# Shorter convolutions, other first loads and a new order of events in a convolution, attention and expert kernel

## What is computed

```python
x = x + conv(_gn(x))                        # per channel of an image: normalise, add a bias, double both axes,
                                            # 12 x 12 filter, leaky relu * sqrt(2), 12 x 12 filter, every second point
t = tokens(x)                               # (16, 1024, 32)
t = t + attention(_ln_t(t), Wq, Wk, Wv)     # one causal head of width 32 over 1024 tokens
u = _ln_t(t)
probs = softmax(u @ gate_w.T + gate_b, axis=tokens)
topv, topi = top_k(probs, 8)                # 8 tokens for each of 16 experts of an image
pooled = sum(topv * u[topi])                # (16 images, 16 experts, 32)
out = gelu([pooled, 1] @ weight1) ... @ weight2
t = t + scatter_add(topi, topv * out)
```

## Time and profile before

| | us |
|---|---|
| median of 3 runs | 413.75 |
| the profiled execution | 406.51 |
| its span in the trace | 404.6 |
| PE busy in it | 348.4 |
| DVE busy | 310.3 |
| ACT busy | 256.4 |
| POOL busy | 239.8 |
| mean granted clock of TensorE | 0.943 |

### The profile page before, as it was taken

How to read it: one execution, slowest core, us unless ns; L and a number is a source line. 1 busy time by engine, 2 the same in 40 slices (tenths; PEclk the granted TensorE clock), 3 DMA queues, 4 the chain that set the end, 5 groups by cost and what they waited for, 6 DMA issues and landing times.

```text
span 404.6 us, 7839 instructions
## 1 busy us (share of the span) xinstructions
PE 348.4 (86%) x3046; PEld 260.4 (64%) x3046; DVE 310.3 (77%) x559; ACT 256.4 (63%) x343; POOL 239.8 (59%) x141
## 2 busy tenths in 40 slices
PE   1189998999899999999599999999986887969775
PEld 1068876667587776857477677676764535647574
DVE  2888779786969878699868786986998995765521
ACT  0113454797988959788476778898696888830500
POOL 5314564366679698886734989856497974162000
PEclk9999999999999999999789999999998997998755
DMA  3900000000000000000000000000020000000311
GB/s 105 203 1 2 2 0 2 2 3 0 3 3 2 0 2 3 2 1 2 0 2 2 2 2 2 2 2 2 0 56 0 2 0 25 19 0 20 86 52 53
DMA packets 16033, 6.70 MB, mean 17 GB/s; under 512 B 6735, under 2 KB 15869, under 8 KB 15997
## 3 DMA queue, kind: packets, MB, share of 16 engines
q1 hardware_dynamic: 13280, 5.55, 5.3%
q10 hardware_dynamic: 2717, 0.66, 1.1%
HBM read 3.63 MB, written 2.11 MB: 14 GB/s over the span
## 4 chain that ended last, share of the span: by engine, by line
PE 58%; DVE 15%; ACT 10%; issue 9%; DMA 3%; POOL 2%; SPq 1%; ACTq 1%; DVEq 0%; POOLq 0%
PE psB L874 13%; PE psA L874 11%; PE psB L989 5%; ACT Pp L582 5%; PE psA L974 4%; PE psB L1010 4%; PE psA L1018 3%; PE psA L1054 3%; DVE negmax L739 3%; PE psA L864 3%; PE psA L1032 2%; DVE Pp L393 2%; DVE xin L682 1%; PE psB L992 1%; ACT e L581 1%
## 5 line engine op out<-in xcount | busy, mean ns | idle before, releaser
L393 POOL TENSOR_TENSOR Pp<-e,Pp 128x1024 f16<-128x1024 f32 x45 | 107.3, 2393 | 11.7 <-ACT Pp L582 11.5
L739 DVE TENSOR_REDUCE negmax<-psA 128x1 f32<-128x512 f32 (+7 forms) x128 | 90.7, 749 | 18.5 <-PE psA L977 17.6
L581 ACT ACTIVATE e<-psB 128x1024 f32<-128x1024 f32 (+1 forms) x80 | 76.7, 958 | 9.9 <-PE psB L992 4.5
L582 ACT ACTIVATE Pp<-psB 128x1024 f16<-128x1024 f32 (+1 forms) x80 | 77.0, 963 | 0.0
L874 PE MATMUL psB<-xin,UU 128*128 128x224 f16 (+1 forms) x480 | 56.6, 277 | 1.1 <-ACT Pp L582 0.6
L974 PE MATMUL psA<-zK,yQ 128*128 128x512 f16 (+1 forms) x192 | 49.2, 340 | 9.0 <-DVE uT L759 4.9
L989 PE MATMUL psB<-yQ,zK 128*128 128x512 f16 (+1 forms) x192 | 49.2, 335 | 6.9 <-ACT Pp L582 3.7
L874 PE MATMUL psA<-y,DD 128*128 128x224 f16 (+1 forms) x480 | 55.1, 273 | 0.0
L874 PEld LDWEIGHTS psB<-xin,UU 128*128 128x128 f16 x480 | 47.1, 99 | 9.5 <-ACT oT L586 1.5
L874 PEld LDWEIGHTS psA<-y,DD 128*128 128x128 f16 x480 | 46.7, 98 | 5.5
L489 POOL TENSOR_TENSOR y<-y 128x1024 f16<-128x1024 f32 x16 | 36.7, 2291 | 14.1 <-ACT y L547 14.1
(11 more groups left out here) (157 smaller groups left out, 603.7 us busy)
## 6 DMA issues: line engine op xcount, KB each, us to landing
x_all<-in_x_dram SPq DMA_DIRECT2D x4, 512.0 KB, 4.6
out_dram<-x_all SPq DMA_DIRECT2D x8, 256.0 KB, 2.3
yQ<-rows SPq DMA_DIRECT2D x32, 2.0 KB
Pp<-filter_tables ACTq DMA_DIRECT2D x4, 121.9 KB, 3.3
w_halves<-y SPq DMA_DIRECT2D x12, 32.0 KB, 1.8
cst<-shape_constants SPq DMA_DIRECT2D x1, 326.5 KB, 4.2
y<-in_L_ffn_weight_dram SPq DMA_DIRECT2D x4, 64.0 KB, 1.9
xin<-in_L_ffn_weight_dram SPq DMA_DIRECT2D x1, 256.0 KB, 3.4
```

The source lines that it names most:

```text
L393: return engine.tensor_tensor(Pp[:, n % 2, 1, o:o + N], e32[:, (NU * n + i) % 3, 0:N], Pp[:, n % 2, 0, o:o + N], ALU.subtract)
L581: nc.scalar.activation(e32[:, m % 3, 0:N], slot(e)[:, 0:N], ACT.Exp)
L582: nc.scalar.activation(Pp[:, n % 2, 0, UOFF[e[2]]:UOFF[e[2]] + N], slot(e)[:, 0:N], ACT.Exp).then_inc(b_drained, 1)
L739: ins = nc.vector.tensor_reduce(negmax[:, n % 2, m - 1:m], s[:, at:at + P * m], X, ALU.max, negate=True)
```

## The change

1. `up`: the two middle output rows (t of 1 and 2) used a matrix for k = -1 and another for k = 1. Those two each have one half of the partitions that is not zero, so they are one matrix now, applied without a shift to a new tile `mix`: the image with its first 64 partitions moved by one position one way and its last 64 the other way. Eight products, 24 matmuls, 18 of them on 256 columns. UU gets its blocks in places that wrap around (`filter_places`).
2. `mix` is filled by DMAs on SP (four for each of two pieces of a group); of the first image by ACT and DVE copies. DVE clears the edge columns (event `edges`, four memsets a group).
3. `down`: four of the ten products have 64 output columns that are not zero. They are issued as pairs of 64-column tiles, one into partitions 0 to 63 and one into 64 to 127, at the end of the pass: 18 full matmuls and 12 halves.
4. Start: the bias of the convolution gets its own semaphore; the gate's bias and x of group 1 are loaded ahead of the wait for the tables; U is made in three events between the statistics of group 0; UU is filled by three DMAs on SP, one copy on ACT and two on DVE; 12 `keep_busy` matmuls stand ahead of the first `up`.
5. Last group: its logits go from PE to ACT to DVE in two halves; ACT calls an exponential of one element at `uT` 3; scatter 0 stands before `wT` 3.
6. A new STEP, FIRST and LAST. `late` lets a later image keep less lead: `up` runs 9 steps ahead for images 0 to 2, 7 for 3 to 5 and 6 from image 6 (before: 5, with the tail of the same step); `down` 7, 5 and 4 from image 3; `prob` units 0 to 2 of an image stand one step earlier; `pv` 14 stands a step later.

The diff, cut to its core:

```diff
+PRODUCTS = ((0, 0), (0, 1), (1, 0))
+LOW, HIGH = slice(0, P // 2), slice(P // 2, P)
-def batch(ahead, name, *more):
+def batch(ahead, name, *more, late=()):
 
-    return lambda t: (name, t + ahead) + more if 0 <= t + ahead < B else None
+    at = {n - ahead + sum(n >= m for m in late): n for n in range(B)}
+    event = lambda t: (name, at[t]) + more if t in at else None
+    return event
...
-FIRST = [("xT", 0), ("gn_mean", 0), ("gn_var", 0), ("U", 0), ("normalise", 0), ("image", 0), ("UU", 0), ("image_low", 0)]
+FIRST = [("xT", 0), ("U", 0), ("gn_mean", 0), ("U", 1), ("gn_var", 0), ("U", 2), ("normalise", 0), ("image", 0), ("image_low", 0), ("edges", 0)]
...
+STEP = [once(-7, "xT", 1), group(5, "uT"), batch(0, "prob", 3), group(4, "mean", 1), once(-3, "image_low", 1),
+        group(3, "mean", 0), once(-4, "xT", 2), once(-5, "small", 1), batch(1, "shift"), once(2, "image", 3),
+        batch(3, "split_z"), batch(0, "low", 2), once(1, "normalise", 3), group(7, "pool"), once(-5, "image", 1),
+        once(21, "dev", 3, 1), once(14, "w1", 1), once(19, "mean", 3, 1), batch(7, "down", late=(1, 1, 3,)),
+        batch(0, "low", 3), batch(2, "score", 1), once(-3, "gn_mean", 2), group(6, "route"), once(-6, "gn_mean", 1),
+        once(-8, "xT", 3), once(5, "edges", 3), batch(0, "zV"), once(-7, "small", 0), group(4, "dev", 1),
+        batch(8, "y_low", late=(1, 3, 6,)), batch(0, "prob", 4), once(-2, "gn_var", 2), group(5, "logits"),
+        group(3, "dev", 0), group(2, "proj", 0), batch(2, "score", 4), batch(3, "zK"), batch(2, "score", 2),
+        batch(1, "prob", 0), once(3, "image_low", 3), once(-9, "dnT", 0), once(-1, "gn_var", 3), batch(0, "low", 4),
+        once(1, "image_low", 2), batch(1, "low", 0), group(5, "logit_max"), once(-5, "normalise", 1),
+        batch(5, "tok", late=(1,)), batch(2, "score", 3), batch(2, "score", 0), batch(1, "prob", 1),
+        once(-3, "gn_mean", 3), batch(4, "z_rstd"), once(-3, "edges", 1), group(5, "logit_exp"),
+        once(-2, "normalise", 2), batch(0, "pv", late=(14,)), batch(1, "low", 1), once(1, "edges", 2),
+        once(12, "w1", 0), group(6, "wT"), once(-6, "gn_var", 1), batch(3, "yQ"), once(15, "proj", 3, 1),
+        batch(1, "prob", 2), once(-4, "small", 2), group(3, "proj", 1), batch(9, "up", late=(3, 3, 6,)),
+        once(0, "image", 2), group(5, "select")]
+
+LAST = [("hidden", 0), ("proj", G - 1, 2), ("mean", G - 1, 2), ("experts", 0), ("dev", G - 1, 2), ("turned", 0),
+        ("uT", G - 1), ("scatter", 1), ("logits", G - 1), ("logit_max", G - 1), ("logit_exp", G - 1),
+        ("select", G - 1), ("scatter", 2), ("route", G - 1), ("scatter", 0), ("wT", G - 1), ("pool", G - 1),
+        ("hidden", 1), ("experts", 1), ("turned", 1), ("scatter", G - 1)]
...
+        def filter_places(r):
+
+            q, far = slice(C * r, C * r + C), max(0, 2 - r)
+            moves = [(R - 1 - r, R - 1 - r + NS, 0, NS)] + ([(0, far, NS - far, NS)] if far else [])
...
             for b in range(GB):
                 sp.dma_start(gw_sb[:, b, :], gate_w).then_inc(proj_loaded, 16)
+                sp.dma_start(gb_sb[E_ * b:E_ * b + E_, :], gate_b.rearrange("(e a) -> e a", a=1)).then_inc(proj_loaded, 16)
+            sp.dma_start(x_all[:, 1, :].rearrange("p (b a n) -> p b a n", b=GB, a=2), x_tokens[1]).then_inc(x_loaded[1], 16)
             sp.wait_ge(toeplitz_loaded, 16 * R)
...
+            sp.wait_ge(fills_ready, 4)
+            sp.wait_ge(U_split, 2)
+            for r in (0, R - 1):
+                spread_filter(sp, r)
...
+                elif name == "image_low":
+                    if g >= 1:
+                        sp.wait_ge(mix_ready, 4 * g)
+                    if g >= 2:
+                        sp.wait_ge(b_filled, BU["up", GB * (g - 1) - 1] + 1)
+                    for i, (lo, hi) in enumerate(PIECES):
+                        if g == 0 and i == 0:
+                            continue
+                        for part, filled in enumerate((xin_high, xin_ready)):
+                            sp.wait_ge(filled, 2 * g + 1 + i)
+                            image, mixed = img[g % 2][part], mix[:, g % 2, part, :]
+                            sp.dma_start(mixed[0:P // 2, lo:hi - 1], image[0:P // 2, lo + 1:hi]).then_inc(mix_moved[i], 16)
+                            sp.dma_start(mixed[P // 2:P, lo + 1:hi], image[P // 2:P, lo:hi - 1]).then_inc(mix_moved[i], 16)
...
                     if g == 0 and i == 0:
-                        pool.wait_ge(filters_loaded, 48)
+                        pool.wait_ge(bias_loaded, 16)
...
+            act.wait_ge(fills_ready, 4)
+            act.wait_ge(U_split, 2)
+            place_to, place_from = filter_places(2)[0]
+            nc.scalar.activation(place_to, place_from, ACT.Copy).then_inc(UU_copied, 1)
...
+                    if n == G - 1:
+                        cut = BANK
+                        act.wait_ge(logits_half, n + 1)
+                        nc.scalar.activation(lg[:, 0:cut], slot(e)[0:GE, 0:cut], ACT.Identity, bias=gb_sb[:, 0:1]).then_inc(lg_half, 1)
+                        act.wait_ge(b_filled, BU[e] + 1)
...
+                elif e == ("uT", G - 1):
+                    act.wait_ge(route_ready, n)
+                    nc.scalar.activation(probs[0:1, 0:1], cst[0:1, 0:1], ACT.Exp)
...
+                    if n == 0:
+                        pe.wait_ge(masks_ready, 3)
+                        keep_busy(s[:, 0:BANK], 12)
                     if n % GB <= 1:
                         pe.wait_ge(xin_ready, 2 * (n // GB) + 1 + n % GB)
                     if n == 0:
-                        pe.wait_ge(UU_ready, R)
-                    parts = [v[:, BC * (n % GB):BC * (n % GB) + BC] for v in img[n // GB % 2]]
-                    for t in range(R):
-                        ins = convolve(s[:, BC * t:BC * t + BC],
-                                       [(UU[:, i, R * k - t + NS - 1, :, :], parts[j], k) for k in (-1, 0, 1) if 0 <= R * k - t + NS - 1 < SPAN
-                                        for i, j in ((0, 0), (0, 1), (1, 0))])
+                        pe.wait_ge(UU_ready, 16 * 3)
+                        pe.wait_ge(UU_copied, 3)
...
+                    for t, matrices in ((0, ((NS - 1, parts, 0), (2, parts, -1))), (3, ((3, parts, 0), (NS, parts, 1))),
+                                        (1, ((NS - 2, parts, 0), (1, mixed, 0))), (2, ((NS - 3, parts, 0), (0, mixed, 0)))):
+                        if t == 1 and n % GB <= 1:
+                            pe.wait_ge(mix_ready, 4 * (n // GB) + 2 + 2 * (n % GB))
+                        ins = convolve(s[:, BC * t:BC * t + BC], [(UU[:, i, m, :, :], v[j], k) for m, v, k in matrices for i, j in PRODUCTS])
...
-                    ins = convolve(s[:, 0:BC], [(DD[:, i, R * k + t + 3, :, :], y_parts[n % 2][j][:, BC * t:BC * t + BC], k) for k in (-1, 0, 1)
-                                                for t in range(R) if 0 <= R * k + t + 3 < SPAN for i, j in ((0, 0), (0, 1), (1, 0))])
+                    for t, k in ((0, 0), (1, 0), (2, 0), (3, 0), (0, 1), (3, -1)):
+                        for i, j in PRODUCTS:
+                            partial(s[:, 0:BC], DD[:, i, R * k + t + 3, :, :], y_parts[n % 2][j][:, BC * t:BC * t + BC], k,
+                                    start=(t, k, i, j) == (0, 0, 0, 0))
+                    for i, j in PRODUCTS:
+                        for pair in (((2, -1, LOW), (1, 1, HIGH)), ((1, -1, LOW), (2, 1, HIGH))):
+                            for t, k, half in pair:
+                                ins = partial(s[half, 0:BC], DD[:, i, R * k + t + 3, half.start // C:half.stop // C, :],
+                                              y_parts[n % 2][j][:, BC * t:BC * t + BC], k, stop=(i, j) == PRODUCTS[-1])
```

137 lines of the change are left out of this document (84 added, 53 removed).

## The result

The kernel after takes 410.98 us (median of 19 runs, 409.07 to 413.36), the kernel before in the same series 406.45 us (19 runs, 405.03 to 414.64). The ratio is 1.012, 95% interval 1.010 to 1.015: the change makes the kernel 1.2% slower, 5.0 us. I forecast 387 us and faster. The times of before fall into two clusters, near 406 and near 413 us; the ratios, and the times of the experiments, leave disturbed executions out.

The account below looks back on a forecast made before the run. PE was taken to set the pace in the loop, DVE next. Convolutions 12.1, start 4.8, slow step 3.5 and end 6.5 sum to 26.9 us, taken from 413.75 us: 387 us, range 375 to 404.

Parts of the forecast that it names:

- The convolutions: `up` and `down` passes: 17.3 us less PE time (9.9 and 7.4), of which 12.1 us become time.
- Rival C: `down`: the halves or their weight loads run one after the other; 394 us, chance 0.08.
- the 70%: Convolutions: share of PE's saved 17.3 us taken to become time, giving 12.1 us; ends 0 and 17.3.
- rival B: Loop: DVE and ACT take over, so only 14.8 us are gained; 399 us, chance 0.19.
- rival D: SP's queue: `mix` DMAs ahead of `shift` hold `prob` 0 for 13.5 us in three groups; 400 us, chance 0.05.
- The slow step: 27.7 us step from 188.3 us, with PE standing behind `image_low` 3: 3.5 us saved; ends 0 and 7.5.
- (a): End: logits in two halves put ACT's copy and maxima beside PE's second product; 1.1 us.
- (b): End: scatter 0 leaves the path between `wT` and `pool` and fills PE's wait; 1.8 us, including the logits' halves.
- (c): End: `proj` 3,1 and image 14's normalisation come ahead of the last `pv`; 2 us.
- (d): End: probabilities run one step ahead, leaving one unit fewer where ACT and DVE bound; 2 us.
- (e): End: without PE's wait the clock, 0.70 over the last 47.6 us, may hold a little longer; 0.7 us.
- E: Loop: PE stands repeatedly and its clock falls, 7.5 us each; gain used up from the fourth stall; chance 0.12.

Follow-up runs that it names:

- experiment 2: Kernel after with passes of 30 full matmuls again in `up` and `down`, new order kept: 423.58 us, ratio 1.043.
- experiment 8: Kernel after without the supply of `mix` and with passes of 30, leaving order, start and end: 417.57 us, ratio 1.028.
- experiment 7: Kernel before, its order and start, with 24 matmuls in `up` (no shift in the middle rows) and the pairs in `down`: 398.22 us, ratio 0.985.
- experiment 14: Kernel before with only the pairs of 64-column tiles in `down`, all results kept: 407.23 us, ratio 1.002.
- experiments 10 and 11: POOL computes only two columns of each low part from image 2 on: in the kernel after 394.83 us, in the kernel before 400.68 us.
- experiment 6: Kernel after without copies, DMAs, memsets and waits for `mix`; middle rows of `up` read the unshifted image: 406.71 us.
- experiment 9: Kernel after with `edges` 0 placed behind `dnT` 0 and 4 useless matmuls instead of 12: 407.18 us, ratio 1.001.
- experiment 16: Kernel before with the new end alone (LAST, logits in two halves, early exponential): 403.66 us, ratio 0.988.
- after, neither: Kernel after without the supply of `mix` and with POOL's low parts cut to two columns from image 2 on: 388.0 us.
- before, no POOL low parts: Kernel before with POOL computing only two columns of each low part from image 2 on: 400.68 us, ratio 0.986.
- experiment 15: Kernel after with the event `pool` alone half a step earlier: 411.45 us, ratio 1.013.

## Why the prediction was wrong

**The convolutions: passes right, their worth near, taken for the result.** `up` 2.79 and `down` 2.91 us as forecast; halves run side by side; 12.6 us by experiment 2 against my 12.1. Rival C is out. That the 70% came out so near is in part luck: the same passes gave 10.9 us in experiment 8 against 6 and 8 in the old order (experiment 7), and the pairs alone nothing (experiment 14). And the term was added to a kernel in which nothing else changed, and the order had.

**"DVE's share goes from 83 to 89%": the number right, the reading wrong.** It is 89% (162.86 of 183.16 us from `shift` 1 to 11), but by luck: the steps are 18.3 us long there, not 16.4, and DVE is busy 5.6 us more than in the same ten steps before (157.25). I read 89% as 11% free. But at least 24.3 us of DVE's busy time in the kernel after are standing still beside POOL's low parts, before 12.9 (experiments 10 and 11). This is the step that failed: my sum held DVE's durations fixed under a new order. The earlier trace rows had the sign of it, 4.81 us for two operations beside 5.37 us of POOL, and I used that row to price one stall and as a hint for rival B, not as a cost that each such operation pays according to what POOL does at that moment. The 10.4 us by which the two kernels differ in experiments 10 and 11 (16.2 - 5.8) are the price of it.

**"I cost them at nothing": the supply of `mix`.** It costs 4.3 us in the kernel after (experiment 6), and 6.8 where POOL does not hide it (394.83 - 388.0). I watched SP's queue for it (rival D). The queue was no trouble; the wait sat on DVE, whose `edges` wait for the DMAs with other work behind them.

**The start, 4.8 us forecast.** The weights came 0.9 us later than I had said (22.79 us, by the start of the pass in experiment 9, against 21.9). I had the 12 useless matmuls run in idle time and end by then. But `dnT`, which stood behind the first pass before, now stands ahead of them and ends near 19.7 us; they ran until 24.57 us and were the path. Leaving most of them out is no cure: in experiment 9 the pass then runs at half its pace and ends later. So the first pass gained 2.3 us, not 4.8. And an earlier first pass is not an earlier `shift` 0: without any supply the first pass ends at 26.46 us, 3.0 us sooner than before, and `shift` 0 comes only 1.8 sooner. The step I left out was to follow what stands behind the first pass, above all the 4.35 us that `edges` 0 waits ahead of the second filter.

**The slow step, 3.5 us forecast.** Right at its place: 19.1 us instead of 27.7, 8.6 us. But I had priced one place alone, and such stalls recurred at two others: at `pool` of the second group (22.8 us with PE idle for 5.22, before 16.9) and at `normalise` 2 (20.2 us with PE idle for 3.93, before 17.4). What the one place gave, these two took, 8.7 us. Experiment 7 shows that short passes do not cure the old one: 27.1.

**The end, 6.5 us forecast.** (a) and (b), 1.8 us, were too small: 2.5 to 2.7 by experiment 16. In the kernel after, the pool product starts 9.6 us behind the end of the logits, where I had forecast 10. (c), (d) and (e) failed. The last `pv` starts 21.2 us behind `shift` 15 (361.57 - 340.34), before 16.5 (351.13 - 334.64). `pv` 14 and the third `pool` stand there in both lists, but DVE is busy 18.2 us in that stretch, before 9.9, since work that the old list has behind the last `pv` has moved ahead of it. From there the kernel needs 13.1 us to `uT`, before 17.6. Together that is 34.3 us against 34.1: (c) moved time and won none, and nothing of (d) shows either. The mean clock behind `shift` 15 is 0.73, before 0.74, so (e) gave nothing, and the logits met the lower level and took 3.25 us against 1.93:

```profile
361.57 0.62 PE L1119 MATMUL psB<-Pp,zV 128*64 128x512 f16 x4
...
374.63 1.09 PE L956 MATMUL psA<-cst,u 128*128 128x128 f32 x8 [1.13 <-DVE u L874]
...
379.68 3.25 PE L1134 MATMUL psB<-uT,gateT 128*64 128x512 f32 x4
```

**The rivals.** B named the engine and E the sign; neither had the price. B let DVE bound the loop and left its work as it was, so it could only lose gain, never make the kernel slower. E wanted four stalls like that of 4.08 us, each with a falling clock, before the gain was gone, and found two (3.93 us at 109.5 and 5.22 at 296.5); the rest of the gain went in waits that it did not have.

**What is left.** With POOL's low parts and the supply gone the change is worth 12.7 us, not 26.9. The stages of that pair (rows "after, neither" and "before, no POOL low parts" of the table) give 0.7 to `shift` 0, 9.3 to 11, 0.8 to 15 and 1.7 behind it. So start and end, forecast at 11.3, were oversized by 8.9 us even without either cost, and convolutions and slow step, forecast at 15.6, by 5.5. With the 10.4 us of POOL and the 6.8 of `mix` this is, within 0.2, the whole miss of 31.4 us. It stays open why the last stage grows when the kernel reaches it sooner: the profiled executions of experiments 9, 14 and 15 lost there 2.5, 2.9 and 5.0 us. In 9 and 14 that comes with a lower clock; what lowers it, and what the 5.0 us of experiment 15 are beside the two waits named there, is not shown.
